# Experts of a mixture layer: the turns and scatters of a group of four batches move between the experts of the next group, on one ring of four PSUM banks shared with the gathers, with the expert outputs held twice

## The reference, cut to what matters

```python
def _L0_ffn_ref(x, router_w, w1, b1, w2, b2):      # x: layernormed, B=32, T=256, D=128, 8 experts
    capacity = max(1, int(Sz * CAP_FACTOR / E) + 1)          # 65
    scores = softmax(einsum('bsd,ed->bse', x, router_w))
    gate_vals, sel_idx = top_k(swapaxes(scores, 1, 2), capacity)   # per batch and expert: 65 tokens
    tokens = x[b_idx, sel_idx]                                # gather
    h = gelu(einsum('becd,edh->bech', tokens, w1) + b1)       # up, hidden 512
    y = einsum('bech,ehd->becd', h, w2) + b2                  # down
    return zeros_like(x).at[b_idx, sel_idx].add(y * gate_vals)  # scatter
x = x + _L0_ffn_ref(_layernorm(x), ...)                       # twice in the program
```

## Time and profile before

| | |
|---|---|
| median of 3 runs | 3567.07 us (3566.18 to 3569.9) |
| profiled execution, own time | 3569.11 us |
| its span | 3567.3 us |
| PE busy | 3112.0 us, 87% of the span |
| DVE / ACT / POOL busy | 2343.9 / 1722.8 / 1199.0 us |
| granted TensorE clock, mean | 0.907 |
| expert stage m0 | about 593 to 952 us |
| expert stage m1 | about 1807 to 2166 us |

### The profile page before, as it was taken

How to read it: one execution, slowest core, us unless ns; L and a number is a source line. 1 busy time by engine, 2 the same in 40 slices (tenths; PEclk the granted TensorE clock), 3 DMA queues, 4 the chain that set the end, 5 groups by cost and what they waited for, 6 DMA issues and landing times. The chain is left out here.

```text
span 3567.3 us, 49293 instructions
## 1 busy us (share of the span) xinstructions
PE 3112.0 (87%) x16500; PEld 2058.4 (58%) x16500; DVE 2343.9 (66%) x5381; ACT 1722.8 (48%) x3723; POOL 1199.0 (34%) x1206
## 2 busy tenths in 40 slices
PE   6999974999872999997579998788889999999989
PEld 2455564888641444444568886676635555555557
DVE  4888875555564777775845553003579999999964
ACT  2444322333341899997133332212356666666644
POOL 3444420000122777775100000001234444444432
PEclk9999966999995999999589996557999999999999
DMA  3000011111032101101221100000000000000001
GB/s 111 1 1 1 1 39 66 37 37 34 17 118 77 30 25 30 30 27 37 62 75 37 45 1 1 0 0 26 1 1 1 1 1 1 1 1 1 1 8 41
DMA packets 106555, 91.23 MB, mean 26 GB/s; under 512 B 15501, under 2 KB 96147, under 8 KB 104000
## 3 DMA queue, kind: packets, MB, share of 16 engines
q1 hardware_dynamic: 104928, 87.25, 7.7%
q10 hardware_dynamic: 1376, 0.82, 0.1%
HBM read 57.60 MB, written 30.15 MB: 25 GB/s over the span
## 5 line engine op out<-in xcount | busy, mean ns | idle before, releaser
L2370 ACT ACTIVATE m_x_hT<-m_x_hid,wm_b 128x260 f32<-128x260 f32 x512 | 242.6, 477 | 433.5 <-PE m_x_hid L2292 433.5
L1319 POOL TENSOR_TENSOR c_tE<-c_tE,c_tDm 128x256 f32<-128x256 f32 x512 | 372.2, 728 | 139.5 <-ACT c_tE L1279 125.7
L1202 DVE TENSOR_REDUCE c_tM<-c_tpa 128x2 f32<-128x512 f32 x512 | 330.0, 681 | 130.9 <-PE c_tpa L1104 129.9
L1279 ACT ACTIVATE c_tE<-c_tpb 128x512 f32<-128x512 f32 x512 | 309.8, 606 | 43.3 <-PE c_tpb L1121 43.3
L2292 PE MATMUL m_x_hid<-m_x_xg,wm_w 128*128 128x260 f32 x1024 | 306.2, 386 | 8.9 <-ACT m_x_hT L2370 5.4
L2300 PE MATMUL m_x_yp<-m_x_hT,wm_w 128*128 128x260 f32 x1024 | 300.7, 383 | 0.0
L1655 POOL TENSOR_TENSOR b_wkv<-b_at,b_rec 128x512 f32<-128x512 f32 x128 | 163.1, 1274 | 306.2 <-DVE b_rec L1591 306.2
L1104 PE MATMUL c_tpa<-c_tK,c_Qm 96*128 96x256 f16 x1024 | 204.7, 283 | 49.9 <-DMA c_Qm<-aug_d 36.8
L2148 POOL TENSOR_TENSOR rstd_all<-m_x_vareps,m_x_neg_half 128x8 f32<-128x8 f32 x16 | 26.4, 1647 | 652.7 <-DVE m_x_vareps L2231 652.7
L1260 ACT ACTIVATE c_tDm<-wc_pos,c_LD 128x128 f32<-128x128 f32 x512 | 209.2, 411 | 21.1 <-PEq L96 21.1
L1121 PE MATMUL c_tpb<-c_Qm,c_tK 101*128 101x256 f16 x1024 | 198.2, 275 | 23.8 <-ACT c_tE L1279 23.5
(11 more groups left out here) (335 smaller groups left out, 7463.4 us busy)
## 6 DMA issues: line engine op xcount, KB each, us to landing
m_x_ir<-idx_d SPq DMA_DIRECT2D x16, 1040.0 KB, 6.7
xn_d<-xn SPq DMA_DIRECT2D x32, 256.0 KB, 2.3
m_x_xs<-xn_d SPq DMA_DIRECT2D x16, 512.0 KB, 4.0
c_tK<-k_d SPq DMA_DIRECT2D x32, 192.0 KB
c_Qm<-q_d SPq DMA_DIRECT2D x128, 48.0 KB
wm_w<-in_m_w SPq DMA_DIRECT2D x2, 2048.0 KB, 9.8
gate_d<-c_pgate SPq DMA_DIRECT2D x16, 256.0 KB
q_d<-c_phi SPq DMA_DIRECT2D x32, 128.0 KB
```

What stands on the lines that cost most here:

```text
L1202: nc.vector.tensor_reduce(out=M[:, u % 2, 2 * h:2 * h + 2], in_=pa[:, h % 2], axis=AX.X, op=ALU.max).then_inc(s["max_done"], 1)
L1279: nc.scalar.activation(E[:, h % 8].rearrange("p a q -> p (a q)"), pb[:, h % 2, :], ACT.Exp).then_inc(s["exp_done"], 1)
L1319: nc.gpsimd.tensor_tensor(diag, diag, Dm[:, u % 2, h:h + 1, :].to_broadcast([P, 2, P]), ALU.mult).then_inc(s["dmul_done"], 1)
L2370: nc.scalar.activation(hT[:, e % 2, j, :], hid[:, c % 2, 0:QW], ACT.Gelu, bias=w["m_b1"][:, c:c + 1]).then_inc(s["gelu_done"], 1)
```

## The change

The tail of quad q is taken apart. Its turns stand in slots 0, 1, 3 and 4 of quad q + 1 and its scatters in slots 2, 4, 5 and 6, after the gather unit of the slot. A ninth pass of the loop, with no experts, does them for the last quad. `yT` is held twice, `ys` three times. One table, `ring`, numbers all units in their order. The five `select` of a batch stand together in slots 0 to 3 of the next quad. `bn` and `moments` come one quad later, and so does `inverse`. The condition of `load` is written with the table; it waits for the same gather as before.

```diff
@@ -2087,8 +2087,9 @@
         oh = sb("oh", [P, 2, 2, SL], F16)
         xg = sb("xg", [P, 2, NE, QB, CAP])
         hT = sb("hT", [P, 2, NJH, QW])
-        yT = sb("yT", [P, QB, NE, CAP])
-        ys = sb("ys", [CH, 2, NCH, D])
+        yT = sb("yT", [P, 2, QB, NE, CAP])
+        YS = 3
+        ys = sb("ys", [CH, YS, NCH, D])
         sel = sb("sel", [CH, QB, NCH, T])
         W2 = 2 * QB
...
-        UNITS = 8 + 3 * QB
-        first_unit = lambda q: q * UNITS + 8
-        tail_order = [("t", 0, 0), ("t", 0, 1), ("t", 1, 0), ("t", 1, 1), ("o", 0, 0), ("t", 2, 0), ("t", 2, 1),
-                      ("o", 1, 0), ("t", 3, 0), ("t", 3, 1), ("o", 2, 0), ("o", 3, 0)]
...
+        TURNS = {0: 0, 1: 1, 3: 2, 4: 3}
+        OUTS = {2: 0, 4: 1, 5: 2, 6: 3}
+
+        ring = {}
+
+        def take_place(unit):
+            ring[unit] = len(ring)
+
+        for unit in range(8):
+            take_place(("g", 0, unit))
+        for q in range(NQ + 1):
+            for e in range(NE):
+                if q + 1 < NQ:
+                    take_place(("g", q + 1, e))
+                if q > 0 and e in TURNS:
+                    take_place(("t", q - 1, TURNS[e], 0))
+                    take_place(("t", q - 1, TURNS[e], 1))
+                if q > 0 and e in OUTS:
+                    take_place(("o", q - 1, OUTS[e]))
+        bank = lambda *unit: ring[unit] % 4
 
         @block.sync
         def _(sp):
-            def load(q, slot, wait):
-                if wait == 2:
-                    sp.wait_ge(s["misc"], 8)
-                if wait > 2:
-                    sp.wait_ge(s["misc"], first_unit(q - 3) + 8)
+            def load(q, slot):
+                if q >= 2:
+                    sp.wait_ge(s["misc"], ring["g", q - 2, 7] + 1)
...
-            for q in range(NQ):
+            for q in range(NQ + 1):
                 if q + 2 < NQ:
                     low_part(q + 2, q % 2)
-                inverse(q)
+                if q > 1:
+                    inverse(q - 2)
+            inverse(NQ - 1)
...
-            def tail(q, number):
-                for i, (kind, b, part) in enumerate(tail_order):
-                    bank = (8 + i) % 4
-                    dve.wait_ge(s["misc"], number + i + 1)
-                    if kind == "t":
...
+            def select(q, b):
+                if q > 0:
+                    dve.wait_ge(s["misc"], ring["o", q - 1, b] + 1)
+                for c in range(NCH):
...
+            def turned(q, b, part):
+                n = q * QB + b
...
+                dve.wait_ge(s["misc"], ring["t", q, b, part] + 1)
+                if part == 0 and n >= YS:
+                    dve.wait_ge(s["misc"], ring["o", (n - YS) // QB, (n - YS) % QB] + 1)
...
+            def out(q, b):
+                dve.wait_ge(s["misc"], ring["o", q, b] + 1)
...
             def bn(q, i0, i1):
                 at_least(dve, s["root_done"], q)
                 if i0 == 0:
-                    dve.wait_ge(s["misc_free"], (first_unit(q) if q == NQ - 1 else first_unit(q) + 8) + len(tail_order))
+                    dve.wait_ge(s["misc_free"], ring["o", q, QB - 1] + 1)
...
+            def quad(q):
+                u = q % 2
+                if q + 1 < NQ:
                     onehot(q + 1, 1 - u, 0)
                 for e in range(NE):
-                    if not first and e in (1, 2):
-                        bn(q - 1, (e - 1) * QB, e * QB)
-                    if not first and e == 3:
-                        moments(q - 1)
-                    if not last and e % 2 == 0 and e // 2 + 1 < QB:
+                    if q > 1 and e in (0, 1):
+                        bn(q - 2, e * QB, (e + 1) * QB)
+                    if q > 1 and e == 2:
+                        moments(q - 2)
+                    if q + 1 < NQ and e % 2 == 0 and e // 2 + 1 < QB:
                         onehot(q + 1, 1 - u, e // 2 + 1)
-                    if not last:
-                        take(1 - u, e, number + e)
-                    for m in range(QB * NCH * e // NE, QB * NCH * (e + 1) // NE):
-                        select(q, m)
-                    y_out(q, e)
-                tail(q, number if last else number + 8)
+                    if q + 1 < NQ:
+                        take(q + 1, e)
+                    if q > 0 and e < QB:
+                        select(q - 1, e)
+                    if q > 0 and e in TURNS:
+                        turned(q - 1, TURNS[e], 0)
+                        turned(q - 1, TURNS[e], 1)
+                    if q > 0 and e in OUTS:
+                        out(q - 1, OUTS[e])
+                    if q < NQ:
+                        y_out(q, e)
...
+            def free(*unit):
+                at_least(pe, s["misc_free"], ring[unit] - 3)
...
+            def turn(q, b, part):
+                if b == 0 and part == 0:
+                    pe.wait_ge(s["y_done"], (q + 1) * NE)
+                free("t", q, b, part)
...
+            def scatter(q, b):
+                n = q * QB + b
+                free("o", q, b)
+                pe.wait_ge(s["sel_done"], (n + 1) * NCH)
+                pe.wait_ge(s["misc_free"], ring["t", q, b, 1] + 1)
...
+            def quad(q):
+                u = q % 2
+                if q < NQ:
+                    for j in range(NJH):
+                        up(q, u, 0, j, q > 0)
                 for e in range(NE):
-                    if not last:
-                        gather(q + 1, 1 - u, e, number + e, True)
-                    for j in range(NJH):
+                    if q + 1 < NQ:
+                        gather(q + 1, e)
+                    if q > 0 and e in TURNS:
+                        turn(q - 1, TURNS[e], 0)
+                        turn(q - 1, TURNS[e], 1)
+                    if q > 0 and e in OUTS:
+                        scatter(q - 1, OUTS[e])
+                    for j in range(NJH if q < NQ else 0):
                         if e + 1 < NE:
                             up(q, u, e + 1, j, True)
-                        down(q, e, j, not first)
```

More of the change, by code:

```diff
@@ L2122, in _ @@
             for q in range(4):
-                load(q, q % 2, q)
+                load(q, q % 2)
                 if q == 1:
@@ L2128, in _ @@
                 for u in range(2):
-                    load(i * 2 + u, u, 4)
+                    load(i * 2 + u, u)
             begin_loads(nc, arrive, loads)
@@ L2173, in onehot, with take @@
                                             ALU.is_equal).then_inc(s["onehot"], 1)
-            def take(slot, unit, number):
+            def take(q, unit):
                 b, er = unit // 2, unit % 2
-                dve.wait_ge(s["misc"], number + 1)
+                dve.wait_ge(s["misc"], ring["g", q, unit] + 1)
                 n = NE // 2
-                nc.vector.tensor_copy(xg[:, slot, er * n:(er + 1) * n, b, :],
-                                      misc[:, unit % 4, 0:n * CAP]
+                nc.vector.tensor_copy(xg[:, q % 2, er * n:(er + 1) * n, b, :],
+                                      misc[:, bank("g", q, unit), 0:n * CAP]
                                       .rearrange("p (e c) -> p e c", e=n)).then_inc(s["misc_free"], 1)
@@ new lines, in turned @@
+            def turned(q, b, part):
+                n = q * QB + b
+                c0, c1 = split[part]
+                dve.wait_ge(s["misc"], ring["t", q, b, part] + 1)
+                if part == 0 and n >= YS:
+                    dve.wait_ge(s["misc"], ring["o", (n - YS) // QB, (n - YS) % QB] + 1)
+                nc.vector.tensor_copy(ys[:, n % YS, c0:c1, :].rearrange("p c d -> p (c d)"),
+                                      misc[0:CH, bank("t", q, b, part), 0:(c1 - c0) * D]).then_inc(s["misc_free"], 1)
@@ L2254, in _ @@
                     onehot(0, 0, unit // 2 + 1)
-                take(0, unit, unit)
+                take(0, unit)
             dve.wait_ge(s["cols_ps"], 1)
@@ L2258, in _ @@
             dve.wait_ge(s["cols"], 1)
[L2259 to L2265, removed]
+            for q in range(NQ + 1):
+                quad(q)
             bn(NQ - 1, 0, W2)
@@ L2270, in _, with gather @@
         def _(pe):
-            def gather(q, slot, unit, number, later):
+            def free(*unit):
+                at_least(pe, s["misc_free"], ring[unit] - 3)
+            def gather(q, unit):
                 b, er = unit // 2, unit % 2
+                slot = q % 2
                 n = NE // 2 * CAP
@@ L2276, in gather @@
                 pe.wait_ge(s["onehot"], 2 * (QB * q + b + 1))
-                if later:
-                    pe.wait_ge(s["misc_free"], number - 3)
+                free("g", q, unit)
                 for h in range(2):
                     for i, part in enumerate((xh, xl)):
-                        mm = nc.tensor.matmul(misc[:, unit % 4, 0:n], lhsT=part[:, slot, 2 * b + h, :],
+                        mm = nc.tensor.matmul(misc[:, bank("g", q, unit), 0:n], lhsT=part[:, slot, 2 * b + h, :],
```

(20 more changed lines are left out.)

26 lines of the change are left out of this document (8 added, 18 removed).

## The result

| | before | after |
|---|---|---|
| median | 3567.54 us (3566.18 to 3569.9, 4 runs) | 3595.12 us (3592.48 to 3601.49, 4 runs) |
| ratio | | 1.0081, 95% interval 1.0066 to 1.0096 |
| profiled execution: own time, span | 3569.11, 3567.3 | 3595.42, 3593.5 |

The change makes the kernel slower by 0.8%, some 28 us. The forecast was 3590, 23 us more than before, with a range of 3578 to 3604.

The account below looks back on a forecast made before the run. The prediction took PE's list to set the stage, with only PE's pauses to be won. Its terms, -18.1 + 21.7 + 12.6 + 3.4 + 3.4 = +23.0 us, gave a median of 3590.1 us, range 3578 to 3604.

Parts of the forecast that it names:

- 14 tails covered: Tails between quads, seven per stage in two stages: PE's waits for y_out and ys vanish, 1.29 us each, -18.1.
- ten casts waiting for loads: Quads 1 to 5 of both stages: ACT's cast waits for ir and PE pauses in slot 0, +21.7 us.
- end of both stages, with their clock: Last quad's tail: DVE's selects, bn and moments delay the last addition, +12.6 us; one clock fall per stage, +3.4.
- clock after the ten pauses: PE's clock falls at two of the ten new pauses, those of load(7), +3.4 us; bounds 0 and 17.
- landing - 4.47: Loss per quad at the cast in quads 1 to 5, from the load's landing time: 1.9 to 2.9 us each.
- rule of the Trainium skill: Transfers take about 2.0 us plus bytes at 436 GB/s, so the ten cast losses would be about 7.6 us.
- the forecast's reading of its rows: PE's clock stayed up after pauses of 2.52 and 1.70 us but fell after 2.90, losing 1.7 us.
- rival with falls at most pauses: PE's clock falls at most new pauses, 1.7 us each, ten giving 3603.7 us; chance 0.2.
- an early load: Rival at the casts: loads come early enough, 3572.6 us, no measurable change; chance 0.05.
- a short end: Rival at the stage end: no longer than before because the waits there overlap, 3574.1 us; chance 0.05.

Follow-up runs that it names:

- kernel with the later cast: Changed kernel with the cast of load(q + 2) two experts later in ACT's list, before slot 3's gelus instead of slot 1's: 3557.37 us.
- late loads: Changed kernel where load(q) waits for one gather unit more, the first of the next quad: 3661.42 us.
- separate semaphore: Changed kernel, cast in its old place but waiting for its own transfer only, xs and ir having semaphores of their own: 3553.5 us.
- kernel with early selects: Changed kernel with the last quad's twenty selects in slots 3, 5, 6 and 7 of its own experts, not the last pass: 3577.73 us.

## Why the prediction was right

The three mechanisms were right. Their sizes, by the terms of the sum, in the one profiled execution of each kernel:

| term | forecast | measured |
|---|---|---|
| 14 tails covered | -18.1 | -18.8: load(3) to load(7) 172.5 for 177.7, from there to the last `y_out` 127.6 for 131.9, in both stages, kernel with the later cast against before |
| ten casts waiting for loads | +21.7 | +22.4: ten pauses, 19.7 in all, and 0.27 of restart each |
| end of both stages, with their clock | +16.0 | +15.5: last `y_out` to last `bn` 22.2 and 19.2 for 12.9 each |
| clock after the ten pauses | +3.4 | +5.0: three falls, 1.6, 1.7 and 1.7 |
| the two quads 0, clock and a longer pause | none | +3.8 |
| outside the two stages | none | -1.5 |
| sum | +23.0 | +26.4; the spans differ by 26.2 |

**The tails.** Both waits went, as the waits of the changed kernel show, and DVE had room for its longer slots. That slots with turns and scatters cost PE nothing beyond their rows is shown by the later cast: 43.13 is the 1.29 less that was worked out. The last quad gains some tenths more.

**The loads.** The step that a tail of 12.4 us had hidden the landing was right, and so was its price, landing - 4.47: 21.7 forecast, 22.4 measured. In quad 1 the cast waited until 632.30, and the next gather began at 635.63, 3.33 us later. The late loads and the separate semaphore bracket it, one making it longer by the delay or more, the other taking it away with the cast where it was. The rule of the Trainium skill ("DMA: Bandwidth & Descriptors", section "Anatomy of one DMA — SWDGE (gpsimd) path"), by which the loss would have been 7.6, does not hold for these transfers on SP's queue: `ir` landed 6.3 us or more after its issue in the changed kernel too.

**The end.** PE's last three scatters began 11.7 us after the last `y_out` (950.24 - 938.58), forecast 11.8, and in m1 the last addition came 18.66 us after the last `y_out`, forecast 18.7 without the clock. With the selects moved out the end is back at 13.15.

**The clock.** This was the weak term. Two falls were taken at the ten pauses, both at load(7); there were three, behind pauses of 2.33, 2.00 and 2.44 us, and none behind the longest, 2.62. So the forecast's reading of its rows, that a pause of 2.52 does not suffice and one of 2.90 does, is no rule: here 2.00 sufficed. The profiled execution of the kernel with early selects, with its ten pauses at the same places, shows three falls as well, behind 2.32, 2.02 and 2.38, and none behind 2.55.

At the ends one fall each was taken for a lone turn part, at 1.7. The clock fell at the first scatter in both stages, after 1.97 us of waiting, and that cost nothing (18.66 in m1, as forecast without a fall); in m0 it fell a second time, at the last three scatters, and that cost 3.0 (9.96 for 6.96). That the 3.0 is near the 3.4 taken is luck.

The term that had been left out is quad 0. Its pause in m0 was 2.52 us in both executions; before, the clock stayed up, and after, it fell. From load(2) to load(3) that made 36.20 for 34.51. In m1 the pause was 3.82 for 2.90, with 38.71 for 36.58. No work moved into quad 0, and the kernel with early selects, which has the same quad 0, took 34.54 and 35.19 there: it is most likely the spread between executions. The same holds for the -1.5 outside the stages.

The rival with falls at most pauses (3603.7) is excluded by the count, three of ten in two profiled executions; those with an early load or a short end by the pauses and by DVE's timeline. What stays open is what decides whether the clock falls at a pause of 2.0 to 2.6 us. No run here tells it.

## What to carry to other kernels

A stretch that looks like waste may be cover for something that is timed by it. Before a tail is dissolved, list every transfer that is started ahead of it and first needed behind it, and set its time to landing against what is left. When work is moved one iteration later, look at the last iteration by itself: what was hidden there has nothing to hide in. A consumer should wait for the transfer that it reads and not for its neighbour on the same semaphore.

## What the runs showed of the hardware that I had not expected

The same pause of 2.52 us at the same place was followed by 2.4 GHz in one execution and by 1.2 GHz in another. The windows of the changed kernel show the granted clock at 1.00 until shortly after PE had resumed at 597.44, and only then at half:

```profile
597.00:598.00 1.00, 0.56 (x3) 1.00 0.00 0
598.00:599.00 1.00, 1.00 (x4) 0.58 0.00 0
599.00:600.00 1.00, 1.00 (x4) 0.50 0.00 0
```

So the price of a short pause is its length plus, at times, 1.6 to 3.0 us that follow it, on work that had been at full pace: 1.6 to 1.7 behind the three pauses of quads 1 to 5 and the one of 2.52 us here, 2.9 behind the one of 3.82 us in quad 0 of m1 (38.71, less 31.74 without a pause, 3.82 and 0.27), and 3.0 at the last three scatters of m0.
